# Second attention of a hybrid block: each head on 32 TensorE rows and a PSUM bank of its own

## What is computed

```python
def _L0_attn_b_ref(encodings, attn_W, attn_b, out_W, out_b):
    B, N, D, H = (1, 512, 128, 16)
    HS = D // H                                   # 8
    b, n, d = encodings.shape                     # 16, 256, 128
    qkv = encodings @ attn_W + attn_b
    qkv = qkv.reshape(b, n, H, 3 * HS).transpose(0, 2, 1, 3)
    q, k, v = jnp.split(qkv, 3, axis=-1)
    scores = jnp.einsum('bhki,bhqi->bhkq', k, q) / math.sqrt(HS)
    mask = jnp.arange(n)[:, None] <= jnp.arange(n)[None, :]
    scores = jnp.where(mask, scores, jnp.float32(NEG_INF))
    prob = jax.nn.softmax(scores, axis=2)
    combined = jnp.einsum('bhkq,bhkl->bhql', prob, v)
    out = combined.transpose(0, 2, 1, 3).reshape(b, n, d)
    return out @ out_W + out_b

x = x + _L0_attn_a_ref(_layernorm(x, axis=-1), ...)
x = x + _L0_ffn_ref(_layernorm(x, axis=-1), ...)      # 8 experts, top 2
x = x + _L0_attn_b_ref(_layernorm(x, axis=-1), ...)
x = x + _L0_ffn_ref(_layernorm(x, axis=-1), ...)
```

## Time and profile before

| | us |
|---|---|
| median of 3 runs (835.46 to 837.83) | 836.0 |
| the profiled execution, its own time | 834.34 |
| its span in the profile | 832.6 |
| TensorE busy | 758.5 |
| VectorE (DVE) busy | 511.0 |
| ScalarE (ACT) busy | 420.8 |
| GpSimd (POOL) busy | 424.4 |

### The profile page before, as it was taken

How to read it: one execution, slowest core, us unless ns; L and a number is a source line. 1 busy time by engine, 2 the same in 40 slices (tenths; PEclk the granted TensorE clock), 3 DMA queues, 4 the chain that set the end, 5 groups by cost and what they waited for, 6 DMA issues and landing times. The chain is left out here.

```text
span 832.6 us, 18673 instructions
## 1 busy us (share of the span) xinstructions
PE 758.5 (91%) x6472; PEld 688.9 (83%) x6472; DVE 511.0 (61%) x1678; ACT 420.8 (51%) x1019; POOL 424.4 (51%) x519
## 2 busy tenths in 40 slices
PE   5787699799999997999999999999989599999994
PEld 4677689799999996777778787787779599999994
DVE  4687764254444466768787888867656344444437
ACT  2455445244444432755766666665655144444455
POOL 3247777155555550423444565665576255555530
PEclk9899979899999999999999999999999799999998
DMA  7981111233433134232223332233011233334138
GB/s 261 315 351 50 48 48 55 71 101 94 121 100 103 56 90 133 89 118 81 77 82 103 115 121 81 78 91 107 20 38 44 66 88 102 94 98 126 55 93 231
DMA packets 78164, 87.42 MB, mean 105 GB/s; under 512 B 12744, under 2 KB 66602, under 8 KB 77944
## 3 DMA queue, kind: packets, MB, share of 16 engines
q1 hardware_dynamic: 67872, 68.60, 26.9%
q0 software_dynamic: 9216, 17.34, 6.3%
q10 hardware_dynamic: 984, 0.29, 0.2%
HBM read 48.59 MB, written 39.65 MB: 106 GB/s over the span
## 5 line engine op out<-in xcount | busy, mean ns | idle before, releaser
L1145 ACT ACTIVATE hT<-bank,bias_T 128x256 f32<-128x256 f32 x448 | 175.4, 475 | 213.3 <-PE bank L788 213.2
L520 POOL DMA_INDIRECT y_rows<-yo,row_cur x160 | 157.6, 985 | 147.2 <-DVE yo L1608 120.4
L1698 DVE TENSOR_REDUCE negp<-bank 128x2 f32<-128x512 f32 (+1 forms) x192 | 128.1, 686 | 55.5 <-PE bank L852 52.9
L809 PE MATMUL bank<-w_s,hT 128*128 128x128 f32 x1280 | 155.9, 275 | 0.0
L809 PEld LDWEIGHTS bank<-w_s,hT 128*128 128x128 f32 x1280 | 150.0, 192 | 0.0
L558 POOL TENSOR_SCALAR_AFFINE_SELECT pt<-pt 128x512 f32<-128x512 f32 x128 | 79.5, 643 | 136.5 <-ACT pt L1205 136.4
L505 POOL DMA_INDIRECT x_slots<-xr,slot_u x128 | 128.8, 1006 | 39.5 <-issue 33.4
L1205 ACT ACTIVATE pt<-bank 128x512 f32<-128x512 f32 x192 | 107.7, 596 | 75.2 <-PE bank L880 62.8
L788 PE MATMUL bank<-xT_hl,w_hl 128*128 128x256 f32 x960 | 136.3, 292 | 3.3 <-DVE w_hl L1581 2.6
L788 PEld LDWEIGHTS bank<-xT_hl,w_hl 128*128 128x128 f32 x960 | 121.5, 193 | 4.0 <-DVE w_hl L1581 3.0
L1608 DVE TENSOR_TENSOR yo<-bank,b_b 128x256 f32<-128x256 f32 x80 | 34.0, 424 | 146.5 <-PE bank L809 146.5
(11 more groups left out here) (199 smaller groups left out, 1237.6 us busy)
## 6 DMA issues: line engine op xcount, KB each, us to landing
xg<-x_slots SPq DMA_DIRECT2D x80, 136.0 KB, 2.2
w_s<-in_L_ffn_w SPq DMA_DIRECT2D x32, 256.0 KB, 3.2
qk_rows<-qks SPq DMA_DIRECT2D x16, 512.0 KB, 4.3
bdk<-qk_rows SPq DMA_DIRECT2D x192, 32.0 KB
qc<-qk_rows SPq DMA_DIRECT2D x48, 128.0 KB, 2.8
x_slots<-xg SPq DMA_DIRECT2D x1, 5440.0 KB, 21.2
y_rows<-xg SPq DMA_DIRECT2D x1, 4096.0 KB, 15.0
bdk<-y_rows SPq DMA_DIRECT2D x1, 4096.0 KB
```

What stands on the lines that cost most here:

```text
L520: pool.indirect_dma_start(y_rows, bass.IndirectOffsetOnAxis(ap=row_cur[:, g % ROWS, j:j + 1], axis=0), yo[:, g % RING, j, :], None, bounds ...
L809: m = pe.matmul(yb(w, l)[:, j * P:(j + 1) * P], hT[:, w % 2, f, j * P:(j + 1) * P], wt[:, f, :], start=(f == 0), stop=(f == FT - 1))
L1145: a = act.activation(hT[:, w % 2, f, :], HB[2 * (w % 2) + f // 2][:, (f % 2) * 256:(f % 2) * 256 + 256], ACT.Silu, bias=bias_T[:, b0 + f:b ...
L1698: dve.tensor_reduce(dst, AB[(g + k) % 2][:, :].rearrange("p (j k) -> p j k", j=heads), AX.X, ALU.max, negate=True).then_inc(S.amax_done, 1)
```

## The change

Each head now has 32 rows of the array and a bank of its own. `kh` and `qh` replace `bdk` and `qc`: head j of a group sits on rows 32 j to 32 j + 23, its negated maximum on row 32 j + 24 of `qh`, facing ones in `kh`. Both have three buffers in place of two. Queries and keys are loaded by 24 transfers a sequence (L394) in place of 15, issued in SP's order behind the transfers of group 2. The maxima no longer reach the query tile by ACT's copy alone: ACT copies them into `negs`, and SP sends them from there into `qh` by two small transfers a unit (`neg_rows`, L403), which the second scores wait for (`neg_in`).

First and second scores are issued together, by `scores(..., k)` in two parts: k = 0 takes the first scores of heads 0 and 1 of unit U+1 (banks 0, 1) and the second scores of heads 2 and 3 of unit U-2 (banks 2, 3); k = 1 takes the other heads, with the banks exchanged. All other TensorE work of a step, transpose and projections, stands between the two, the values of U-3 behind the second. DVE's maxima and ACT's exponentials go by two heads at a time. The load of zeros into `bdk` and its rows of ones go.

```diff
-            def restack(t, par):
+            def split_heads(t, par):
                 n = 2 * t + par
...
                 sp.wait_ge(S.hilo_done, n + 1)
-                need(sp, k_in, 16 * 12 * t)
-                need(sp, q_in, 48 * t)
-                sp.dma_start(qk_rows[par], qks[:, par, :, :, :].bitcast(F32)).then_inc(rows_stored, 16)
-                sp.wait_ge(rows_stored, 16 * t + 16)
-                need(sp, S.c_done, 3 * GRP * (n - 1))
+                need(sp, qk_in[(n - 2) % 3], 16 * QK_LOADS * ((n - 2) // 3 + 1))
+                sp.dma_start(qk_rows[par], qks[:, par, :, :, :].bitcast(F32)).then_inc(qks_stored[par], 16)
+                sp.wait_ge(qks_stored[par], 16 * t + 16)
+
+                need(sp, S.c_done, 2 * GRP * (n - 2))
                 rows = qk_rows[par].rearrange("(g r) a b t -> r g a b t", g=GRP)
-
-                for part, half in enumerate((0, 1, 0)):
-                    for j in range(4):
-                        r = HD * j
-                        sp.dma_start(bdk[32 * part + r:32 * part + r + HD, par, :, j, :].bitcast(F32), rows[r:r + HD, :, half, 1, :]
-                                     ).then_inc(k_in, 16)
-                for part, half in enumerate((0, 0, 1)):
-                    sp.dma_start(qc[32 * part:32 * part + 32, par, :, :].bitcast(F32), rows[:, :, half, 0, :]).then_inc(q_in, 16)
+                for dst, which, halves in ((kh, 1, (0, 1, 0)), (qh, 0, (0, 0, 1))):
+                    for part, half in enumerate(halves):
+                        for j in range(4):
+                            r = 32 * j + HD * part
+                            sp.dma_start(dst[r:r + HD, n % 3, :, :].bitcast(F32), rows[HD * j:HD * j + HD, :, half, which, :]
+                                         ).then_inc(qk_in[n % 3], 16)
+
+            def neg_rows(t, par, g):
+
+                n, U = 2 * t + par, 2 * GRP * t + GRP * par + g
+                sp.wait_ge(S.neg_set, U + 1)
+                need(sp, S.c_done, 2 * (U - 3))
+                for c in range(2):
+                    sp.dma_start(qh[8 * PARTS:P:32, n % 3, g, c * P:c * P + P].bitcast(F32), negs[c:P:32, g % 2, :].bitcast(F32)).then_inc(neg_in[U % 4], 16)
 
             def attn_b_pair(i):
                 for h in range(2):
-                    if valid(i + 3):
-                        y_load(i + 3, h)
-                    if valid(i + 1):
-                        restack(i + 1, h)
+                    for g in range(GRP):
+                        if valid(i):
+                            neg_rows(i, h, g)
+                        if g == 1 and valid(i + 3):
+                            y_load(i + 3, h)
+                        if g == 2 and valid(i + 1):
+                            split_heads(i + 1, h)
...
+            def scores(t1, p1, g1, t2, p2, g2, k):
...
+                U1, U2 = 2 * GRP * t1 + GRP * p1 + g1, 2 * GRP * t2 + GRP * p2 + g2
+                n1, n2 = 2 * t1 + p1, 2 * t2 + p2
+                first, second = (2 * k, 2 * k + 1), (2 - 2 * k, 3 - 2 * k)
+                if valid(t1):
+                    if g1 == 0 and k == 0:
+                        pe.wait_ge(qk_in[n1 % 3], 16 * QK_LOADS * (n1 // 3 + 1))
+
+                    need(pe, S.amax_done, 2 * (U1 - 1) + k + 1)
+                    need(pe, S.exp_done, 2 * (U1 - 3) + k)
+                if valid(t2):
+                    if k == 0:
+                        pe.wait_ge(neg_in[U2 % 4], 32 * (U2 // 4 + 1))
+                    pe.wait_ge(S.amax_done, min(2 * (U2 + 3) + k, 2 * UNITS))
+                    need(pe, S.exp_done, 2 * (U2 - 1) + k + 1)
+                for wide in (True, False):
+                    if valid(t1):
+                        for j in first:
+                            q = qh[32 * j:32 * j + 8 * PARTS, n1 % 3, g1, :]
+                            keys = kh[32 * j:32 * j + 8 * PARTS, n1 % 3, g1, :]
+                            if wide:
+                                pe.matmul(bank[j][:, P:3 * P], q[:, P:SEQ], keys, start=True, stop=False)
+                            else:
+                                pe.matmul(bank[j][:, 0:P], q[:, 0:P], keys[:, 0:P], start=False, stop=False)
+                    if valid(t2):
+                        for j in second:
...
+                            if wide:
+                                m = pe.matmul(bank[j][:, P:3 * P], keys[:, 0:P], q, start=True, stop=True)
+                            else:
+                                m = pe.matmul(bank[j][:, 0:P], keys[:, P:SEQ], q[:, P:SEQ], start=True, stop=True)
+                if valid(t2):
+                    m.then_inc(S.c_done, 1)
+                if valid(t1):
+                    for j in first:
+                        m = pe.matmul(bank[j][:, 0:3 * P].rearrange("p (c k) -> p c k", c=3)[:, 0:3:2, :], ident_r[:, :],
+                                      cmask[:, :].unsqueeze(1).broadcast_to([P, 2, P]), start=False, stop=True)
+                    m.then_inc(S.a_done, 1)
...
             def neg_copy(t, par, g):
                 U = 2 * GRP * t + GRP * par + g
                 act.wait_ge(S.negT_done, U + 1)
-                act.activation(qc[96:P, par, g, :], MB[96:P, 0:SEQ], ACT.Copy).then_inc(S.neg_set, 1)
+                need(act, neg_in[(U - 2) % 4], 32 * ((U - 2) // 4 + 1))
+                act.activation(negs[:, g % 2, :], MB[:, 0:P], ACT.Copy).then_inc(S.neg_set, 1)
...
             def max_b(t, par, g, k):
...
-                dve.tensor_reduce(dst, AB[(g + k) % 2][:, :].rearrange("p (j k) -> p j k", j=heads), AX.X, ALU.max,
-                                  negate=True).then_inc(S.amax_done, 1)
+                dst = negp[:, g % 2, :].rearrange("p (j r) -> p j r", r=32)[:, 2 * k:2 * k + 2, :]
+                both = front_banks[:, 2 * k:2 * k + 2, :]
+                dve.tensor_reduce(dst[:, :, 0], both[:, :, 0:P], AX.X, ALU.max, negate=True)
+                dve.tensor_reduce(dst[:, :, 1], both[:, :, P:3 * P], AX.X, ALU.max, negate=True).then_inc(S.amax_done, 1)
```

More of the change, by code:

```diff
@@ L42 @@
 LAYERS = 2
+PARTS = 3
+QK_LOADS = 2 * PARTS * GRP
+UNITS = GRP * SEQS
 LEAD, SECOND, PLACED = 5, 8, 5
@@ L166, in build @@
         yab = sb("yab", [P, 2, 4, D])
-        v_ext = sb("v_ext", [P, 2, 2, HEADS, 32])
-        negp = sb("negp", [P, 2, 2, P])
+        negp = sb("negp", [P, 2, P]); negs = sb("negs", [P, 2, P], F32R)
         cmask = sb("cmask", [P, P], F32R); ident_r = sb("ident_r", [P, P], F32R)
@@ L288, in build @@
         y_back = [sem(f"y_back{k}") for k in range(PAIRS)]
+        qks_stored = [sem(f"qks_stored{k}") for k in range(2)]
+        qk_in = [sem(f"qk_in{k}") for k in range(3)]
+        neg_in = [sem(f"neg_in{k}") for k in range(4)]
         slots2 = (S.slots2_even, S.slots2_odd)
@@ L553, in causal @@
                 U = 2 * GRP * t + GRP * par + g
-                pool.wait_ge(S.exp_done, 3 * U + 3)
-                first = pt[:, g % 2, 0:2, :].rearrange("p u (j q) -> p (u j) q", j=2)[:, :, 0:P]
-                second = pt[:, g % 2, 2, :].rearrange("p (j q) -> p j q", j=4)
-                for blk in (first, second):
-                    a = pool.affine_select(out=blk, in_=blk, compare_op=ALU.is_ge, fill=0.0, base=0,
-                                           pattern=[[0, 4], [1, P]], channel_multiplier=-1)
-                a.then_inc(S.aff_done, 1)
+                for k in range(2):
+                    pool.wait_ge(S.exp_done, 2 * U + k + 1)
+                    blk = pt[:, g % 2, 1 - k, 0:2, :, :].rearrange("p c j q -> p (c j) q")
+                    pool.affine_select(out=blk, in_=blk, compare_op=ALU.is_ge, fill=0.0, base=0,
+                                       pattern=[[0, 4], [1, P]], channel_multiplier=-1).then_inc(S.aff_done, 1)
             def add_ob(i):
@@ L860, in neg_transpose @@
             def neg_transpose(t, par, g):
                 U = 2 * GRP * t + GRP * par + g
[L862 removed]
+                pe.wait_ge(S.amax_done, 2 * U + 2)
                 need(pe, S.neg_set, U)
[L864 to L882 removed]
+                pe.transpose(MB[:, 0:P], negp[:, g % 2, :], ident[:, :]).then_inc(S.negT_done, 1)
@@ L1005, in attn_b_pair @@
                             o_back(t, par)
+                        scores(*ahead, *behind, 1)
+                        if valid(g3[0]):
+                            values(*g3)
             def attn_b_end():
                 t, n = PAIRS - 1, 2 * PAIRS - 1
-                neg_transpose(t, 1, 3)
-                pass2(t, 1, 2, 0)
-                pass2(t, 1, 2, 1)
+                scores(PAIRS, 0, 1, t, 1, 2, 0)
                 values(t, 1, 1)
-                pass2(t, 1, 2, 2)
+                scores(PAIRS, 0, 1, t, 1, 2, 1)
                 on_transpose(t, 0)
-                pass2(t, 1, 3, 0)
-                pass2(t, 1, 3, 1)
+                scores(PAIRS, 0, 2, t, 1, 3, 0)
                 values(t, 1, 2)
-                pass2(t, 1, 3, 2)
+                scores(PAIRS, 0, 2, t, 1, 3, 1)
                 r_transpose(n - 1)
                 counts(n - 2, MB)
```

(17 more changed lines are left out.)

130 lines of the change are left out of this document (30 added, 100 removed).

## The result

The changed kernel takes 1028.4 us in the median (1023.2 to 1032.4), the kernel before 835.7 beside it: a ratio of 1.230, with a 95% interval of 1.224 to 1.236. The forecast was 980, from 915 to 1035. The direction and the place were as forecast; the time is 48 us above the centre.

A forecast was written before the change was run, and what follows sets the result against it. TensorE's own work was taken to bound the second attention. A sequence would take 27.0 us (two steps of 4.8, 1.0 for the clock, 16.4 for SP's queue) against 17.4; 146 us over 834.3 gave 980, range 915 to 1035.

The forecast's parts named there:

- About 7 us, once a sequence: TensorE's wait for the transfers of group 3's maxima, behind a store and 24 loads on SP; 14 waits.
- The chain of 16.4: From step 4n+3 to step 4n+5: split 1.15, wake-up 0.1, store 3.9, loads 8.75, maxima's transfers 2.5; 14.0 to 21.0 us.
- Values and projections stand in DVE's time and cost little.: In each second-attention step, this TensorE work fits while DVE reduces the maxima; no time was added for it.
- A half step of 2.4, a step of 4.8.: Bank handover between TensorE and DVE: products 1.0, drain 0.27, reductions 1.1, release 0.04; a step 3.8 to 5.4 us.
- S: Time of TensorE's ten products in half a step, taken as 1.0 us, from 0.5 to 1.3.
- I add 1.0 us a wait: After each sequence's wait, the next step runs partly at TensorE's lower clock: 1.0 us, from 0.5 to 2.
- POOL's wider fill of `kh` in idle time: At the start, POOL's larger fill was counted as nothing, since POOL idles there.
- the bytes' pace: Rival: SP's 24 loads issue in 5.4 us, not 8.75; a sequence takes 23.6, some 935 us; chance 0.10.
- The banks alone: Rival: SP's queue holds nothing up, only shared banks cost, 61 steps at 4.8 us; some 870 us; chance 0.06.
- The low and high ends of S: Rival: as forecast, but the ten products take 0.5 us (about 940) or 1.3 (about 1005); together 0.35.

The follow-up runs named there:

- e5: The changed kernel with the 24 loads issued eight at a time behind the maxima of groups 3, 0 and 1, none behind the store: 967.1 us, ratio 1.159.
- e7: The changed kernel with the maxima's two transfers issued by ACT behind its exponentials, the 24 loads left together on SP: 960.8 us, ratio 1.149.
- e6: e5 with the values and the work of neighbouring sequences moved behind the second part of scores: 985.0 us, ratio 1.178.
- e2: The changed kernel with the values and the work of neighbouring sequences behind the second part of scores, SP's queue unchanged: 1034.7 us, ratio 1.241.
- e9: e6 with four unused products of 128 columns between the two parts of each step: ratio 1.070.
- e10: e6 with the scores' products on all 128 rows and exponents scaled to a thousandth, so it computes something else: ratio 1.153.
- e8: e7 with the values and the work of neighbouring sequences moved behind the second part of scores: 978.0 us, ratio 1.177.
- e12: The changed kernel with twelve unused products ahead of the wait for the maxima's transfers and four between the parts of every step: ratio 1.250.

## Why the prediction came out as it did

The added time, in the three stretches of the sum (profiled spans, before to after):

| stretch | forecast | measured |
|---|---|---|
| to the start of step 2 (332.39, now 353.83) | 9.0 | 21.4 |
| steps 2 to 57 (240.0, now 401.3) | 132.2 | 161.2 |
| step 57 to the end (260.2, now 272.0) | 5 | 11.9 |
| all | 146 | 194.5 |

The two marks in between, steps 2 and 57 of after:

```profile
353.83 0.58 PE L863 MATMUL front_banks<-kh,qh 24*128 24x256 f32 x2 [3.81 <-DMA qh<-negs]
...
755.08 0.58 PE L863 MATMUL front_banks<-kh,qh 24*128 24x256 f32 x2 [2.74 <-DMA qh<-negs]
```

The steps of the working, as the prediction put them:

- **"About 7 us, once a sequence", 14 waits.** The mechanism is right: 15 waits for `qh<-negs`, the 14 forecast and one at the start, before step 2, and e5 and e7 take them away with 61 and 68 us. The size is half, 3.1 us in the mean (1.1 to 6.2, where 5 to 9 was forecast), since the steps ahead of the wait were longer than forecast.
- **The chain of 16.4.** Measured 17.3. That it came so near is luck in part, since its terms were off in both directions: the wake-up with the split 0.85 and not 1.25, the store 2.6 and not 3.9, the 24 loads 8.3 and not 8.75, the two transfers 5.5 and not 2.5. The last, and its mean of 4.9 too, lies outside the bound of 4.5 that I had put on it. L395, the nearest row, was one transfer of 128 KB; the two of 2 KB take 1.04 to issue and another 4.5 to the release. No run separates the landing from what SP's 24 loads in flight add to it.
- **"Values and projections stand in DVE's time and cost little."** This step failed. Output work between the halves doesn't only fill DVE's time, it waits for DVE: `on` (26.1 us in all), `x` (12.0), the router's `S_` (9.2), `v_s` (13.6 over three lines), about 61 us of waits of which nothing was in the sum. The two free steps of a sequence took 12.4 us (489.91 to 502.35) and not 10.6; a sequence took 29.0 in the mean and not 27.0. But e6 shows that putting the work elsewhere doesn't win this back by itself.
- **A half step of 2.4, a step of 4.8.** Right, at the upper clock: half a step is 2.20, a step 4.89 in e2 and 5.09 in e9 with its added products. S was 0.82 and not 1.0, with more than half of it in the two masks: 0.43 (500.54 to 500.97), where one took 0.12.
- **"I add 1.0 us a wait"** for the clock. This step failed. I counted the lower clock for one half step in each sequence; the lower one holds for much of the stage, 0.64 to 0.73 in the windows. Half steps without side work are 2.2 at the upper clock and 2.7 to 2.8 at the lower (476.81 to 479.54). With the queue free the clock is worth 0.108 of the time before (e6 and e9).
- **The start.** I took "POOL's wider fill of `kh` in idle time" for nothing. The first store came at 322.69 and not 315.06. POOL's fills (in part) and DVE's casts at that place, from the timelines of after:

```profile
306.21 2.65 POOL L547 MEMSET kh<- 128x3072 f32 x1
...
309.53 1.31 POOL L550 MEMSET v_ext<- 128x1472 f32 x1
```

```profile
302.16 3.25 DVE L1489 CAST xT_hl<-xnT_all 128x256 fp32r<-128x256 f32 x1
...
306.12 5.02 DVE L1489 CAST xT_hl<-xnT_all 128x256 fp32r<-128x256 f32 x1
```

  29 of the 32 casts of this kind take 0.26 to 0.40 us; the two here took 1.3 each before the change, 5.6 us less together. The longer one ends at 311.1, just behind the last of the fills (311.0); TensorE's next products wait behind it. That POOL caused it is read from the overlap, and no run tested it. The Trainium skill, "SBUF — State Buffer", SBUF: two separate sides, says that DVE in a two-port mode and GpSimd exclude each other from a shared pair of ports for a whole instruction. The trace agrees in that the cast and the fills end together; it doesn't show why the cast should have waited for several POOL instructions and not for one. The rest of the 21.4: the second store landed in 6.5 us (334.02 to 340.54) and not in 3.9, and the transfers took 5.1 and not 2.5.

The chances were right in that slower was nearly certain. Of the rivals, the bytes' pace (935) is refuted by the rows of SP's queue: 24 loads take 8.2 us and more, where it had 5.4. "The banks alone" (870) is refuted by e5 and e7 as the case of this kernel, and it is wrong as a price too: with the queue free they take 961 to 967. The low and high ends of S weren't what moved the time: S was under its centre, and the kernel slower than it.

What stays open. How the last 0.07 of e9 splits up: its steps take 5.09 against 4.35, which over 63 is 47 us of some 62; the start is a likely part of the rest, but there is no trace of the kernel before at its 883.7 us. No run put first and second scores on banks of their own again with the row groups kept. Whether the side work costs less between the parts or behind at the upper clock wasn't tried, nor what part of e10's higher clock comes from its products no longer overlapping, nor why e6 and e8 are slower than e5 and e7. No version beat the kernel before.

## What to carry to other kernels

Before a small transfer that the critical path waits for is given to a queue, write down everything that is issued ahead of it: here 24 loads that nobody needed soon cost 61 to 68 us, and moving two issues to another engine took that away. A loop in which two engines hand the same banks to and fro pays every handover; work put between its halves can itself wait for the engine that is busy there (61 us here), but putting it elsewhere only brought other waits (e6, e8), so try it before counting on it. Count the clock as a price of the whole stage, not of one wait: when short waits and narrow products replace dense ones, read the granted clock, and test it by filling the gaps with unused work. But see in the trace whether that work ends before the wait does: in e12 it didn't, and the run says nothing on the clock. And remove causes together as well as singly, since one wait hides another: e2 won nothing with the queue in place.

## What the hardware showed that I had not expected

- Two transfers of 4 rows by 128 values, 2 KB each, cost 0.50 us each to issue, more than the 0.34 of a 32 KB load of 8 rows; behind 24 loads they released TensorE 3.0 to 6.0 us after the first issue, 4.9 in the mean of 15.
- At nearly the same busy share the clock was 0.67 with products on 24 and 25 rows (81%, e6) and 0.93 with the same products on 128 rows and one after the other (79%, e10); with unused products in the gaps it was 1.00 (90%, e9). Unused work won 0.108 of the time.
- Products on separate row groups do run side by side: eight are issued in 0.39 us (500.15 to 500.54); the two masks on all rows behind them take 0.43.
- A cast of 128 by 256 on DVE that takes 0.28 us in most places of the trace lasted 5.02 beside fills by POOL.
